# Four blocks side by side instead of two in the block-diagonal operands of a packed attention

## What is computed

```python
def _L0_xattn_ref(q, k, v):           # x: (16, 256, 256), 4096 tokens of 256; k = v = ctx
    hd = D // NHEADS                  # 16 heads of 16
    scores = jnp.einsum('bsqd,bskd->bsqk', qh, kh) / math.sqrt(hd)   # 16 x 16 for each token
    scores = jnp.where(tril_mask, scores, NEG_INF)
    return jnp.einsum('bsqk,bskd->bsqd', softmax(scores), vh)
x = x + _L0_xattn_ref(_layernorm(x), ctx, ctx)
# then a mixture of 8 experts (256 -> 1024 -> 256) over _layernorm(x), each token to its top-1 expert
x = x + _L0_ffn_ref(_layernorm(x), gate_w, gate_b, w1, b1, w2, b2)
```

## Time and profile before

| | before |
|---|---|
| median of 3 runs | 480.92 us |
| span of the profiled execution | 492.6 us |
| TensorE busy (matmul / weight load) | 402.1 / 338.3 us |
| VectorE, ScalarE, GpSimd busy | 346.3, 177.5, 208.7 us |
| DMA | 105162 packets, 69.39 MB; 78077 of them under 512 bytes |

### The profile page before, as it was taken

One profiled execution on the slowest core, in us unless ns is written; L12 is line 12 of the kernel. 1 busy time (PEld: TensorE's weight loads), 2 busy tenths in 40 slices (PEclk: granted clock), 3 DMA queues, 4 the chain that ended last, 5 costly groups with the idle time before them and its releaser, 6 DMA issues.

```text
span 492.6 us, 16316 instructions
## 1 busy us (share of the span) xinstructions
PE 402.1 (82%) x5967; PEld 338.3 (69%) x5967; DVE 346.3 (70%) x777; ACT 177.5 (36%) x317; POOL 208.7 (42%) x213
## 2 busy tenths in 40 slices
PE   0135868888888866897999999779999999999992
PEld 0025757887787765896887877557778877877871
DVE  7978969789945863477757877457666666766662
ACT  3343255542624221342434433224333333433420
POOL 8345374334673467523723242642333323233221
PEclk9999999999999999975699999889999999999998
DMA  8999578899685664377612232544333322222210
GB/s 282 414 305 218 135 170 241 212 259 260 160 220 119 152 167 107 106 173 181 207 45 67 68 76 81 185 131 155 90 68 77 77 62 62 69 60 61 84 31 0
DMA packets 105162, 69.39 MB, mean 141 GB/s; under 512 B 78077, under 2 KB 88190, under 8 KB 104576
## 3 DMA queue, kind: packets, MB, share of 16 engines
q1 hardware_dynamic: 75696, 56.67, 41.9%
q10 hardware_dynamic: 25984, 3.21, 4.6%
q0 software_dynamic: 3408, 8.46, 4.6%
HBM read 48.28 MB, written 12.57 MB: 124 GB/s over the span
## 4 chain that ended last, share of the span: by engine, by line
PE 55%; DMA 11%; SPq 9%; DVE 9%; issue 6%; POOL 5%; ACT 2%; ACTq 1%; another core or an unknown queue 1%; POOLq 0%; DVEq 0%
PE s_ps L1229 20%; SPq L305 8%; PE at_ps L1245 6%; DMA arena<-qv_hl 6%; PE pv_ps L1245 6%; PE pv_ps L1143 6%; PE s_ps L1111 3%; PE lg_ps L1171 3%; PE pv_ps L1246 3%; PE at_ps L1246 3%; POOL qv_hl L987 2%; PE tr_ps L1156 2%; DMA arena<-x 2%; PE st_ps L1196 2%; POOL k_hl L995 1%
## 5 line engine op out<-in xcount | busy, mean ns | idle before, releaser
L1229 PEld LDWEIGHTS s_ps<-arena 128*128 x1872 | 132.7, 99 | 52.2 <-issue 14.6
L1229 PE MATMUL s_ps<-arena 128*128 128x128 f16 x1872 | 158.6, 222 | 8.4 <-DVE arena L906 5.1
L915 DVE SCALAR_TENSOR_TENSOR arena<-arena,s_ps 128x512 f32<-128x512 f32 x78 | 53.6, 687 | 48.6 <-PE s_ps L1229 35.9
L1076 POOL DMA_INDIRECT result<-arena x39 | 38.8, 995 | 95.5 <-DVE arena L940 91.6
L1111 PEld LDWEIGHTS s_ps<-k_hl,arena 128*128 128x128 f16 x1536 | 54.3, 118 | 29.9 <-DMA arena<-qv_hl 22.1
L1111 PE MATMUL s_ps<-k_hl,arena 128*128 128x16 f16 x1536 | 54.7, 179 | 23.3 <-DMA arena<-qv_hl 19.3
L1143 PE MATMUL pv_ps<-a_hl,arena 128*128 128x16 f16 x1536 | 54.7, 179 | 19.7 <-DMA arena<-qv_hl 15.9
L1143 PEld LDWEIGHTS pv_ps<-a_hl,arena 128*128 128x128 f16 x1536 | 53.5, 118 | 22.8 <-DMA arena<-qv_hl 18.3
L1245 PE MATMUL at_ps<-arena,k_in 128*128 x160 | 60.9, 383 | 0.8 <-DVE k_hl L926 0.6
L1245 PE MATMUL pv_ps<-arena,x_in 128*128 x152 | 58.1, 383 | 0.1
L1069 POOL TENSOR_TENSOR arena<-arena 128x256 f32<-128x256 f32 x39 | 30.7, 786 | 60.7 <-DMA arena<-b 60.6
(11 more groups left out here) (143 smaller groups left out, 614.2 us busy)
## 6 DMA issues: line engine op xcount, KB each, us to landing
arena<-w SPq DMA_DIRECT2D x28, 512.0 KB, 6.1
arena<-sorted_rows SPq DMA_DIRECT2D x39, 130.0 KB, 2.4
arena<-b SPq DMA_DIRECT2D x39, 128.0 KB
arena<-qv_hl SPq DMA_DIRECT2D x70, 64.0 KB, 3.5
k_in<-k_t SPq DMA_DIRECT2D x16, 256.0 KB, 3.9
v_in<-v_t SPq DMA_DIRECT2D x16, 256.0 KB
arena<-x SPq DMA_DIRECT2D x4, 1024.0 KB, 12.1
o_sb<-x_r SPq DMA_DIRECT2D x16, 256.0 KB, 3.8
```

The lines of the kernel that those rows point to most:

```text
L915: eng.scalar_tensor_tensor(out=h_in[:, c].rearrange("p (k t) -> p k t", t=P), in0=bias, scalar=W_SCALE, in1=h_ps[c][:].rearrange("p (k t) ...
L1076: eng.indirect_dma_start(out=out, out_offset=bass.IndirectOffsetOnAxis(ap=rows[:, r, :].bitcast(I32)[:, D + 2:D + 3], axis=0), in_=rows[:, ...
L1229: k = eng.matmul(o, weights_of(j, w + k_ * H + n * P, P), xt[:, j % 2, k_ * P:(k_ + 1) * P], start=k_ == 0 and w is HI_1 and xt is xt_hi, ...
```

## The change

`SIDE = 4` blocks stand side by side where two did. `qv_hl` becomes `[P, 3, BLK // 4, HEADS, 4, 2]`, and so do the diagonals: same bytes, half as many runs of 256 bytes (16 columns x 4 blocks x 2 parts x 2 bytes), and the columns of one matrix 16 bytes apart instead of 8. The host lays `x_t` and `v_t` out to match, and the views of `x_in`, `v_in` and of the layer norm's scale and shift follow. The number of DMAs, matmuls, waits and due times is the same.

```diff
-        qv_hl = sb("qv_hl", [P, 3, BLK // 2, HEADS, 2, 2], F16)
+        qv_hl = sb("qv_hl", [P, 3, BLK // SIDE, HEADS, SIDE, 2], F16)
-        SLOT_BLOCKS = BLK // 2
-        diagonals = of_expert(E - 1, 3).rearrange("p (b m u a) -> p b m u a", m=8 * HEADS, u=2, a=2)
+        SLOT_BLOCKS = BLK // SIDE
+        diagonals = of_expert(E - 1, 3).rearrange("p (b m u a) -> p b m u a", m=8 * HEADS, u=SIDE, a=2)
-                    eng.copy(halves(q_hl[i % 2], 0), x_in[:, i % 2, :].rearrange("p (b q u) -> p b q u", u=2, q=HEADS)
+                    eng.copy(halves(q_hl[i % 2], 0), x_in[:, i % 2, :].rearrange("p (b q u) -> p b q u", u=SIDE, q=HEADS)
-                    scale, shift = [st_ps[:, g % 2, n, UNITS * c:UNITS * (c + 1), :].rearrange("p u (b w) -> p (u b) w", w=2)
-                                    .unsqueeze(2).to_broadcast([P, BLK // 2, HEADS, 2]) for n in range(2)]
+                    scale, shift = [st_ps[:, g % 2, n, UNITS * c:UNITS * (c + 1), :].rearrange("p u (b w) -> p (u b) w", w=SIDE)
+                                    .unsqueeze(2).to_broadcast([P, BLK // SIDE, HEADS, SIDE]) for n in range(2)]
-                            m = eng.matmul(s[:, n], q_bd[i % 2][:, n // 2, :, n % 2, q], k_hl[:, n, k, :],
+                            m = eng.matmul(s[:, n], q_bd[i % 2][:, n // SIDE, :, n % SIDE, q], k_hl[:, n, k, :],
-                            m = eng.matmul(o[:, n], v_bd[i][:, n // 2, :, n % 2, v], a_hl[:, n, a, :],
+                            m = eng.matmul(o[:, n], v_bd[i][:, n // SIDE, :, n % SIDE, v], a_hl[:, n, a, :],
-        "x_t": lay(np.transpose(np.reshape(x, by_q_pair), (1, 5, 0, 2, 4, 3))).reshape(P, T * D // P),
+        "x_t": lay(np.transpose(np.reshape(x, by_q_side), (1, 5, 0, 2, 4, 3))).reshape(P, T * D // P),
```

More of the change, by code:

```diff
@@ L25 @@
 CT = 256
+SIDE = 4
 SKIPPED_ROW = 1 << 20
@@ L492, in values @@
                         act.wait_ge(*values_landed(i - 1))
-                    eng.copy(halves(v_hl, 0), v_in[:].rearrange("p (b d u) -> p b d u", u=2, d=HD)).then_inc(s_v_hi, 1)
+                    eng.copy(halves(v_hl, 0), v_in[:].rearrange("p (b d u) -> p b d u", u=SIDE, d=HD)).then_inc(s_v_hi, 1)
             def spread_first_queries():
@@ L663, in queries @@
                     g, c = i // CG, i % CG
-                    q = x_in[:, i % 2, :].rearrange("p (b q u) -> p b q u", u=2, q=HEADS)
-                    scale, shift = [st_ps[:, g % 2, n, UNITS * c:UNITS * (c + 1), :].rearrange("p u (b w) -> p (u b) w", w=2)
-                                    .unsqueeze(2).to_broadcast([P, BLK // 2, HEADS, 2]) for n in range(2)]
+                    q = x_in[:, i % 2, :].rearrange("p (b q u) -> p b q u", u=SIDE, q=HEADS)
+                    scale, shift = [st_ps[:, g % 2, n, UNITS * c:UNITS * (c + 1), :].rearrange("p u (b w) -> p (u b) w", w=SIDE)
+                                    .unsqueeze(2).to_broadcast([P, BLK // SIDE, HEADS, SIDE]) for n in range(2)]
                     yield (27.6, 24.8, 36.4, 45.3, 62.6, 59.0, 78.2, 84.6, 108.8, 115.5, 128.4, 136.1, 154.6, 141.2,
@@ L986, in queries @@
                     q = q_hl[i % 2]
-                    eng.tensor_tensor(halves(q, 1), x_in[:, i % 2, :].rearrange("p (b q u) -> p b q u", u=2, q=HEADS),
+                    eng.tensor_tensor(halves(q, 1), x_in[:, i % 2, :].rearrange("p (b q u) -> p b q u", u=SIDE, q=HEADS),
                                       halves(q, 0), ALU.subtract).then_inc(s_q_lo, 1)
@@ L1002, in values @@
                     pool.wait_ge(s_v_hi, i + 1)
-                    eng.tensor_tensor(halves(v_hl, 1), v_in[:].rearrange("p (b d u) -> p b d u", u=2, d=HD),
+                    eng.tensor_tensor(halves(v_hl, 1), v_in[:].rearrange("p (b d u) -> p b d u", u=SIDE, d=HD),
                                       halves(v_hl, 0), ALU.subtract).then_inc(s_v_lo, 1)
@@ L1260 @@
     lay = np.ascontiguousarray
-    by_unit, by_q_pair, by_v_pair = (T // 64, 8, 8, HEADS, HD), (T // 64, 8, 4, 2, HEADS, HD), (T // 64, 4, 2, 8, HEADS, HD)
+    by_unit = (T // 64, 8, 8, HEADS, HD)
+    by_q_side, by_v_side = (T // 64, 8, 8 // SIDE, SIDE, HEADS, HD), (T // 64, 8 // SIDE, SIDE, 8, HEADS, HD)
     arrays = {
         "x": lay(x).reshape(T, D),
-        "x_t": lay(np.transpose(np.reshape(x, by_q_pair), (1, 5, 0, 2, 4, 3))).reshape(P, T * D // P),
+        "x_t": lay(np.transpose(np.reshape(x, by_q_side), (1, 5, 0, 2, 4, 3))).reshape(P, T * D // P),
         "x_r": lay(np.transpose(np.reshape(x, (T // 8, 8, HEADS, HD)), (1, 3, 0, 2))).reshape(P, T * D // P),
         "k_t": lay(np.transpose(np.reshape(ctx_1024, by_unit), (1, 4, 0, 2, 3))).reshape(P, T * D // P),
-        "v_t": lay(np.transpose(np.reshape(ctx_1024, by_v_pair), (3, 4, 0, 1, 5, 2))).reshape(P, T * D // P),
+        "v_t": lay(np.transpose(np.reshape(ctx_1024, by_v_side), (3, 4, 0, 1, 5, 2))).reshape(P, T * D // P),
         "gate_w": lay(np.tile(np.transpose(np.reshape(L0_ffn_gate_w, (E, HEADS, HD)), (2, 1, 0)), (8, 1, 1))).reshape(P, HEADS * E),
```

## The result

The changed kernel takes 535.20 us, the median of 4 runs (534.71 to 537.06), against 480.07 us (477.74 to 481.33) before. The ratio is 1.113, 95% interval 1.106 to 1.120: slower by 55 us. The forecast was 538.

A forecast was written before the change was run, and what follows sets the result against it. In the attention, the spreading loop (some 10.7 us a turn) and TensorE (10.1 us a chunk) stood close together. Loads +82, filled waits -18, clock -7: +57 on 480.9, 538 us; own range 501 to 558, with rival A's middle 467 to 558.

The forecast's parts named there:

- Where the time lies: All that can move lies in the attention, 21 to 240 us; the stage after 245 us is untouched.
- The loads' pace: Matmuls of scores and outputs: stationary columns 16 bytes apart double the reading, 33.3 to 60 ns each, bounds nothing to 66.7.
- The work: Slower loads add 82 us of TensorE work, 79 of it between 37 and 240 us.
- What the idle time takes up: In the attention, 18 of TensorE's 23.9 us of spreading waits are filled; the other 17.5 us of idle time stay.
- The clock: TensorE in the attention runs mostly at 1.2 GHz; denser work may be granted 2.4, giving back 7 us, at most 11.
- The sum: Whole kernel: 82 - 18 - 7 = +57 us, 538 us; own case's chance 0.54.
- The lower end of my range: Half the surcharge on the loads, 41 us, with the same given back: about +20 us, 501 us.
- The spreading: Spreading DMAs in the attention: half as many runs, twice as long, win 1.2 us a chunk; alone 9 us, bounds 2 and 14.
- A: Loads of scores and outputs cost nothing more, only the spreading counts: 472 us, 467 to 479; chance 0.33.
- B: Loads stay, spreading is bound by issues and the landing's fixed part: 481 us, 479 to 483; chance 0.07.
- C: Loads only partly dearer, some 45 ns, adding 36 us, at most 24 hidden: about 497 us; chance 0.06.

The follow-up runs named there:

- the curve: Kernel before, each chunk's matmuls of scores and outputs reading stationary columns at its own distance, 2 to 96 bytes: 27 ns a matmul at 2, 33 at 8, 60 at 16.
- the run of the spreading alone: Changed kernel, but matmuls of scores and outputs read their stationary columns 8 bytes apart, as before; spreading still in runs of 256 bytes: 476.76 us, ratio 0.988.
- the two half runs: Kernel before with stationary columns read 16 bytes apart in outputs only, 508.86 us (ratio 1.054), or in scores only, 505.82 us (ratio 1.048).

## Why the prediction was right, point by point

**Where the time lies: right.** All of the loss but 0.9 us is in the attention, and the chain passes from the spreading to scores and outputs.

**The loads' pace: right by a choice between bounds, and to the nanosecond in part by luck.** I took 60 ns, and 60.0 was measured. The reason given, "the reading doubles", is only what happens between 8 and 16 bytes; what the curve shows is a price for each 16-byte piece touched, which goes from 64 to 128 pieces. Two steps of the working do not carry the figure. It set the 16 moving columns at 6.7 ns, their time at 2.4 GHz, though it held the attention to run mostly at 1.2 GHz, where by the same reckoning they are 13.3 ns and the sum is 53 ns. And the 20 ns that it gives for the step from 2 to 8 bytes compare durations of loads (medians 105 and 118 ns, 13 apart), where the pace rises by 6 ns. The rule of the Trainium skill ("SBUF — State Buffer", section "Specifications") that speaks of 16-byte lines led to the right side; the trace agrees with the lines and not with "two hits" as the threshold, since 6 to 8 bytes already cost 5 ns and 8 to 10 another 7. The Trainium skill's note on a stride "for free" over 8 bf16 (same page, section "Door 1: The DMA port swizzle"), read as 16 bytes, is contradicted for these loads: 16 bytes cost 60 ns against 27. The duration of a load was mis-sized: I named 145 ns, it shows 170, though the pace rose by 26.7 ns only.

**The work: right.** 79 us in the stage were forecast, 78.7 came.

**What the idle time takes up: too small, at the term put at nothing.** I let 18 us of waits be filled and the other 17.5 us stay; idle time fell by 25.7. The 18 were near: the spreading's waits fell by 22.2 us and the wait for the softmax weights rose by 5.9, 16.3 net. What did not stay is the rest. The waits for routing, for the scaled weights and for keys fell by 10 us, which fits engines beside TensorE that had more room in a longer stage.

**The clock: wrong.** I took 7 us back for a clock that a denser TensorE would be granted. The transposes of the softmax weights, all of them, in the kernel before and in the changed one, and those of the outputs in the changed kernel between 60 and 190 us:

```profile
L1129 PE MATMUL at_ps<-ident,a_sb x64: 417/421/477, 43.7 to 231.9; 128*128 128x128 f32 x64
...
L1130 PE MATMUL at_ps<-ident,a_sb x64: 417/418/477, 45.6 to 280.3; 128*128 128x128 f32 x64
...
L1157 PE MATMUL tr_ps<-ident,o_sb x32: 276/418/477, 106.0 to 189.0; 128*128 128x128 f32 x32
```

418 ns is their duration at 1.2 GHz; at 2.4 GHz, at 249 us, those of the outputs had a median of 277 ns. So TensorE stayed mostly at the lower level in both kernels, and in the changed one it was busy for 94% of the stage. The PEclk column says 0.81 for the stage only because it has full speed up to about 190 us, against these transposes, as it had before; from 192 us to the end of the attention it says 0.52. The clock gave nothing back.

**The sum: right in its total, not in its terms.** 18 + 7 = 25 us were to be given back, and 25.7 were, all of it idle time. The error of the clock (7 us too much) and that of the idle time (8 us too little) cancel, so that +57 against +55 is better than its terms. The lower end of my range was added up wrongly: 41 us with the same 25 given back is +16 and 497 us, not +20 and 501. It changes nothing here.

**The spreading: right in kind, half in size.** Packets fell by 32768 to 72394, 19.8 ns were measured for 19 estimated, the median of SyncE's issues fell to 616 ns (named: 609 to 690), the landing's by 0.5 us in the changed kernel and by 0.2 where the loads stayed at 33 ns. Alone the spreading is worth 5 us, not 9: 0.9 us a chunk were won where 1.2 were taken, and in how many turns that shortened anything no run shows. Beside the slower loads it is worth nothing that can be measured.

**The rivals.** A (the loads cost nothing) is refuted by the pace; had it held, the change would have won 1.2%, as the run of the spreading alone shows. B holds for neither part. C's premise, a pace of some 45 ns, is refuted by the pace. Its sum let 16 to 24 of 36 us hide; of the 41 us in the two half runs 13 and 16 hid, so it would have come out at its upper end or above.

## What to carry to other kernels

The distance of stationary columns is a price on every weight load: where few moving columns follow a load, look at the pace of the matmuls against what their columns take, and count the 16-byte pieces that a load touches (here the price began between 6 and 8 bytes). A layout that interleaves more matrices to lengthen DMA runs buys its gain with that price, and the two meet in one product here (a run is 16 columns times their distance). When two resources stand close together, idle time does not absorb new work first and in full: of 41 us added, about a third hid, and of 82 about a third again, while some 16 us taken away gave nothing.

## What the runs showed of the hardware that was not expected

- 128 stationary f16 columns with 16 moving ones: 33 ns at 8 bytes apart, then 3.4 ns more a byte up to 60 ns at 16, flat beyond but for 67 at 48 and 65 at 96 bytes; 26 to 28 ns at 2 to 6 bytes. The pace at 8 bytes is the same at either level of the clock: 33.6 ns at 70 us, where the mask's matmul of 512 columns takes 586 ns, and 33.3 ns at 213 us, where it takes 379.
- With the same 64 KB a DMA, the median of SyncE's issue of a spreading DMA is 601 ns at 128 descriptors of 512 bytes, 616 at 256 of 256, 742 to 812 at 512 of 128 and 1197 at 1024 of 64, with a minimum near 600 in all. ScalarE's queue shows no such order: 632, 633 to 728, 652 to 948 and 695 ns. What makes the issues longer was not measured by itself.
- TensorE stayed mostly at 1.2 GHz through 250 us in which it was busy for 94%: each of the 64 transposes of the softmax weights took 417 ns or more.
